# Second attention of a two-layer graph network: one addition moved from VectorE to GpSimd, its two readers one step later

## The reference, cut to what matters

```python
a = ex / denom[tgt]
msg = (v[src] + e) * a[..., None]
out = jax.ops.segment_sum(msg, tgt, num_segments=n).reshape(n, HID)
x_r = h @ Wskip + bskip
beta = jax.nn.sigmoid(jnp.concatenate([out, x_r, out - x_r], axis=-1) @ Wbeta)
return beta * x_r + (1.0 - beta) * out          # h of the next step, then batch norm over all nodes
```

## Time and profile before

| | |
|---|---|
| median of three runs | 2253.55 us |
| profiled execution, its own time | 2257.49 us |
| span of its instructions | 2255.7 us |
| busy: PE, DVE, ACT, POOL | 87%, 73%, 58%, 52% |
| mean granted clock of PE | 0.949 |
| second half of attention 1, first `spread` to last bn_stats | 1277.4 to 1401.7 us of the span |
| POOL instructions in that stretch | none |

### The profile page before, as it was taken

How to read it: one execution, slowest core, us unless ns; L and a number is a source line. 1 busy time by engine, 2 the same in 40 slices (tenths; PEclk the granted TensorE clock), 3 DMA queues, 4 the chain that set the end, 5 groups by cost and what they waited for, 6 DMA issues and landing times. The chain is left out here.

```text
span 2255.7 us, 31284 instructions
## 1 busy us (share of the span) xinstructions
PE 1957.4 (87%) x7584; PEld 1106.5 (49%) x7584; DVE 1641.7 (73%) x3493; ACT 1311.9 (58%) x2509; POOL 1183.5 (52%) x919
## 2 busy tenths in 40 slices
PE   3899999989996889888588697599998999599997
PEld 2444444444332444444233232477776777355554
DVE  6799999967698799999233698577776776355553
ACT  3688888852221677777233211577877776466662
POOL 7566566428840433333688000555555555688885
PEclk9899999999798999999789899699999999799999
DMA  6888888744121999999544132999999997755531
GB/s 174 248 264 258 252 255 258 228 144 95 28 54 32 330 367 363 371 356 337 153 116 122 42 110 87 278 308 319 322 321 305 317 322 221 181 123 127 129 102 26
DMA packets 285896, 476.09 MB, mean 211 GB/s; under 512 B 82181, under 2 KB 158866, under 8 KB 285593
## 3 DMA queue, kind: packets, MB, share of 16 engines
q1 hardware_dynamic: 235494, 440.94, 62.0%
q0 software_dynamic: 46400, 33.03, 7.3%
q10 hardware_dynamic: 3824, 0.13, 0.1%
HBM read 272.01 MB, written 202.55 MB: 210 GB/s over the span
## 5 line engine op out<-in xcount | busy, mean ns | idle before, releaser
L390 POOL DMA_INDIRECT first_x<-in_x,first_index x200 | 262.9, 1315 | 158.5 <-ACT first_xn L584 86.0
L1003 POOL TENSOR_TENSOR last_xh<-last_xin,last_hin 125x512 f32<-125x512 f32 x100 | 127.1, 1272 | 223.7 <-DMA last_xin<-in_x 223.7
L785 POOL DMA_INDIRECT second_entry<-node_map,second_si x100 | 129.9, 1299 | 203.3 <-DVE src_row L800 180.3
L1087 PE MATMUL last_psH<-last_g,W2a 128*128 128x500 f32 x400 | 190.9, 600 | 24.4 <-DVE last_hid L1049 24.3
L1096 PE MATMUL last_psO<-W2b,last_hid 128*125 128x128 f32 x1600 | 190.9, 273 | 0.0
L1096 PEld LDWEIGHTS last_psO<-W2b,last_hid 128*125 128x125 f32 x1600 | 182.5, 188 | 0.9 <-issue 0.9
L203 ACT ACTIVATE last_xn<-last_x,last_nb,last_rstd 125x128 f32<-125x128 f32 x400 | 164.0, 487 | 0.1
L544 PE MATMUL first_psW<-first_h,W_in 128*128 128x500 f32 x300 | 153.5, 594 | 0.0
L1138 POOL DMA_INDIRECT out<-elast_o,elast_ends x100 | 128.5, 1285 | 45.1 <-issue 43.5
L856 PE MATMUL second_psZ<-second_h,gate_h 128*128 128x500 f32 x200 | 105.6, 610 | 51.5 <-DVE second_y L811 28.9
L1382 ACT ACTIVATE att_sig<-att_bank,gate_b 128x500 f32<-128x500 f32 x50 | 33.9, 678 | 196.0 <-PE att_bank L1325 196.0
(11 more groups left out here) (288 smaller groups left out, 5079.1 us busy)
## 6 DMA issues: line engine op xcount, KB each, us to landing
hT<-first_h SPq DMA_DIRECT2D x100, 250.0 KB
yT<-first_y SPq DMA_DIRECT2D x100, 250.0 KB
second_yin<-yT SPq DMA_DIRECT2D x50, 500.0 KB
second_hin<-hT SPq DMA_DIRECT2D x50, 500.0 KB
yT<-second_y SPq DMA_DIRECT2D x50, 500.0 KB
last_yin<-yT SPq DMA_DIRECT2D x50, 500.0 KB
first_x<-in_x SPq DMA_DIRECT2D x100, 224.0 KB
h_rows<-second_rows SPq DMA_DIRECT2D x50, 448.0 KB
```

Source lines behind the costliest of these rows:

```text
L390: pool.indirect_dma_start(x[:, to % X, j], None, a["x"], bass.IndirectOffsetOnAxis(index[:, end, r % 2, j:j + 1], 0), bounds_check=last_no ...
L785: pool.indirect_dma_start(entry[:, q], None, scratch.node_map, bass.IndirectOffsetOnAxis(si[:, q], 0), bounds_check=last_node, oob_is_err= ...
L1003: pool.tensor_tensor(xh[:, q % 4], xin[:, q], hin[:, q], ALU.add).then_inc(m.xh, 1)
L1087: last = pe.matmul(psH[h][:, 0:CH], w.W2a[:, 0, h * 128:(h + 1) * 128], g[:, q % 2], start=True, stop=True)
```

## The change

In attention 1 the addition dx = dx + o is taken from DVE and given to POOL (`add_out`, after all its gathers). The mask of run ends and the bn_stats become a stage of their own, `end_of_run`, which runs with lag 1 in attention 0 (where it stood) and with lag 2 in attention 1. DVE gets two more waits, in both attentions: the scan of chunk k waits for the sum of chunk k - 2 (`y`), and 1532 waits for the masked result of chunk k - 2 (`yn`).

```diff
+                def add_out(k):
+                    pool.wait_ge(m.gx, made(k))
+                    pool.tensor_tensor(dx[:, k % 2], dx[:, k % 2], o[:, k % 2], ALU.add).then_inc(m.y, 1)
+
                 steps(C, [(0, fetch if l else scatter)])
+                if l == 1:
+                    steps(C, [(0, add_out)])
...
                     dve.wait_ge(m.gated, made(k - 2))
                     dve.wait_ge(m.pv, made(k))
                     dve.wait_ge(m.o, made(k - 1))
+                    dve.wait_ge(m.y, made(k - 2))
                     dve.tensor_tensor_scan(o[:, s], run_cont[:, q, 0:CH], pv[:, s], o[:, 1 - s, CH - 1:CH] if k else 0.0,
                                            ALU.mult, ALU.add).then_inc(m.o, 1)
 
                 def combine(k):
 
                     s, q = k % 2, k % U
+                    dve.wait_ge(m.yn, made(k - 2))
...
-                    dve.wait_ge(m.gx, made(k))
-                    dve.tensor_tensor(dx[:, s], dx[:, s], o[:, s], ALU.add).then_inc(m.y, 1)
+                    if l == 0:
+                        dve.wait_ge(m.gx, made(k))
+                        dve.tensor_tensor(dx[:, s], dx[:, s], o[:, s], ALU.add).then_inc(m.y, 1)
+
+                def end_of_run(k):
+                    s, q = k % 2, k % U
                     dve.wait_ge(m.y, made(k))
                     dve.scalar_tensor_tensor(out=yd[:, k], in0=run_cont[:, q, 1:CH + 1], scalar=-1.0, in1=dx[:, s], op0=ALU.add, op1=ALU.mult).then_inc(m.yn, 1)
                     dve.wait_ge(m.yn, made(k))
                     dve.bn_stats(w.ends[:, k * 6:k * 6 + 6], yd[:, k]).then_inc(m.ystats, 1)
 
-                steps(C, [(0, weigh), (0, total), (1, combine)])
+                steps(C, [(0, weigh), (0, total), (1, combine), (1 + l, end_of_run)])
```

## The result

| | before | changed | ratio, 95% interval |
|---|---|---|---|
| median (runs) | 2254.28 us (7) | 2237.27 us (7) | 0.9935 [0.9909, 0.9961] |
| profiled execution, span | 2255.7 us | 2234.0 us | |
| first gate of attention 1 to the next phase's first bn_aggr (line 637) | 122.26 us | 108.56 us | |
| from there to the end | 851.0 us | 843.9 us | |

The ratio is worth 14.7 us of 2254.28, between 8.8 and 20.5 us by its interval. The changed median of 2237.27 us lies in the forecast range of 2236 to 2246. The stretch that the change touches is read more sharply: 13.70 us shorter, against 13.65 predicted. The two spans differ by another 8.0 us. Of these, 7.1 lie behind line 637 and 0.9 ahead of the first gate. The code from line 637 to the end is the same in the thirteen kernels of this study, and in their traces it took 839.0 to 853.7 us, so 7.1 us there cannot be put down to the change.

A forecast was written before the change was run, and what follows sets the result against it. DVE bounds attention 1 before, PE after: -14.75 us of steps and +1.10 of tail give -13.65, with +0.75 in attention 0 -12.9 us. Forecast median 2240.7 us (-0.57%), its own range 2236 to 2246, overall 2235 to 2253.

The forecast's parts named there:

- DVE sets the old step, PE the new one: Attention 1: the bound passes from DVE at 4.84 us a step to PE at 4.19; chance 0.65.
- PE's pace of 4.19 us: Attention 1: five products of 0.84 us a step, read where PE did not wait yet, carry all gates.
- The short idle time before 1540: Sign expected in attention 1's profile after: DVE briefly idle before 1540, ended by PE or ACT.
- DVE's own step: Attention 1 after the change: DVE's instructions take 4.01 us a step, 4.06 with the added waits.
- The size of a wait: Added DVE wait at the scan, already met: 0.03 to 0.05 us each, bounds nothing and 0.2 us.
- Attention 0: DVE stays the bound there; the added scan wait, 25 times 0.03 us, costs 0.75 us, at most 5.
- POOL's addition: Attention 1: held behind 1557, it ends 2.46 us after 1540's start, before the scan at 2.83.
- The cover: Attention 1: POOL's sum reaches the scan with 0.26 us to spare; another 0.13 us hides under PE's step.
- the second rival: Attention 1: POOL gets in first and holds 1557, DVE's step becomes 5.3 us, total 2266 us; chance 0.09.
- C + 0.81: Attention 1: 0.81 us after 1540's start (C), when POOL can start; a mask starting later would be held 1.25 us.
- The tail: End of attention 1: the last mask waits for POOL, 2.57 us after the last 1532 instead of 1.47; +1.10 us.
- The loads: Attention 1: `run_cont` loads, issued a step later, keep 2.0 us to spare and cost nothing.

The follow-up runs named there:

- e3: Kernel before the change with product 1327 and the waits for it left out in attention 1; ratio 0.9997, step 4.81 us.
- e2: Changed kernel with product 1327 and the waits for it left out in attention 1; ratio to the kernel before 0.9909, step 3.96 us.
- e1: Changed kernel with a wait and three one-column memsets on DVE ahead of each mask in attention 1; ratio to the kernel before 0.995, step 4.22 us.
- the runs with 250 and 500 columns: Changed kernel with an extra POOL addition of that many columns ahead of each add_out in attention 1; ratios to the kernel before 0.9931 and 0.9999.
- e6: Changed kernel with a wait and one 161-column memset on DVE ahead of each mask in attention 1; ratio to the kernel before 0.9941, step 4.31 us.
- e9: Changed kernel with two 161-column memsets, each waited for, on DVE ahead of each mask in attention 1; ratio to the kernel before 1.0074.
- e4: Changed kernel with mask and statistics back at lag 1 in attention 1, the addition still on POOL; ratio to the kernel before 1.0099.

## Why the prediction was right

**DVE sets the old step, PE the new one.** Right, and shown by e3 and e2: the same product is worth 1.2 us of phase before, most of it from elsewhere, and 7.4 us after. PE's pace of 4.19 us, read from the few steps before PE began to wait, held over the phase: the gates of chunks 0 and 24 stand at 1281.56 and 1381.32, 99.76 us apart, for 24 x 4.19 - 0.84 = 99.72. The granted clock was 1.00 from 1290 to 1380. The short idle time before 1540, ended by PE, came as predicted.

**DVE's own step.** 4.01 us and the waits, 4.06 predicted. Worked out from what was measured: 1540 to the mask 0.63 us in e2, as predicted, the gap 0.30 with six waits, so 4.01 + 0.07 = 4.08 us, which e1 shows as well; 3.96 us in e2 with five waits. The size of a wait was off: 0.07 us for `y` as the sixth instead of 0.03 to 0.05, and nothing for it as the fifth. In attention 1 this cost nothing, since PE's step covers it.

**Attention 0** got 0.39 us longer from its first scan to its last statistics (133.34 to 133.73 us), against 0.75 predicted. This term was sized at twice what it measured, and it is made up otherwise. The gap was not 0.23 to 0.26 us but 0.30 in chunks 2 to 10 and 0.19 late. Eight steps are 0.07 us longer, one where the gap turns to 0.19 is 0.42 longer (5.26 us, the scan waiting for PE's 1325), the late ones are 0.01 to 0.02 shorter, and a step of 5.94 us that the kernel before has near the end is 5.58.

**POOL's addition.** Hold behind 1557, end at 2.42 (2.46 predicted) and the scan after it: as worked out. The start at exactly 0.81 us after 1540 is in part luck: 1540 takes 0.74 us there instead of 0.71, and the handoff 0.07 instead of 0.10. The handoff back took 0.13 us to the scan in the runs with 250 and 500 columns and 0.03 at the last mask, for 0.11 predicted. The cover was 0.46 us by the run with 250 columns, for 0.26 on VectorE and 0.13 under PE in the prediction.

**The decision point of the second rival** was mis-sized. I put it at the start of POOL's row, C + 0.81. e6 shows POOL still losing with the mask at C + 0.93, e9 shows it winning with the mask at C + 1.34. The rival's mechanism is real, with 0.57 us of hold in e9, but it was farther from the changed kernel than I gave it. An estimate of where it decides: POOL's row takes 1.24 us alone and ends 1.10 us after the mask that holds it, so it is 0.14 us into its row when it needs what the mask holds. That fits e6, where the mask started 0.13 us into the row and was first, and the earlier trace rows, where 0.31 us was too late. It puts the decision at C + 0.95. No run has a mask between C + 0.93 and C + 1.34, so this is not shown more closely.

**The tail** cost 0.97 us for 1.10 predicted: 0.08 from the handoff, the rest from a POOL row that ended 1.09 us after the mask's instead of 1.15.

**The loads** of `run_cont` never show in the waits: right by the rows, though not tried by itself.

**The total.** Forecast -12.9 us, measured -14.7 by the ratio, with an interval of 8.8 to 20.5; the two stretches that the change touches sum to -13.70 + 0.39 = -13.3 us. From 1532 or 1540 of chunk 0 to that of chunk 24 the traces give -14.70 for -14.75. That the phase agrees to 0.05 us is partly luck, since small errors offset each other: this term is 0.05 us too favourable, the tail 0.13 too large, and 0.03 lie in stretches that the forecast takes as unchanged. The 0.36 us of the long step are in the forecast too, since it subtracts from the end that the kernel before reached with it. That it came out clear of 0.5% in the median was the likeliest case, but the interval's upper end, 0.9961, does not exclude 0.4%.

The Trainium skill, "SBUF — State Buffer", section "Who interferes with whom", says that issue order decides who blocks. e9 agrees: 1.24 us of POOL untouched, 1.24 instead of 0.67 for the mask. e6 adds that the start of POOL's row in the profile is not the moment at which that order is settled.

No version here that does the whole work is faster than the changed kernel clear of the noise. The next gain would have to take work off PE in this phase, and would meet DVE's own 4.08 us a step after 0.11 us: 24 x 0.11 = 2.6 us. e2 got more in the steps, 24 x 0.23 = 5.5 us, only because a wait on DVE went with the product.

## What to carry to other kernels

Moving an instruction from the bounding engine to an idle one pays only if the bounding engine's own next reader is put far enough behind: 5.52 us a step with the reader at once, 4.19 with the reader a step later. Before summing the gain, look for a stretch in which the second-busiest engine does not wait yet; its pace there is the floor (0.65 us a step gained here, not the 0.78 that DVE gave up). And list the instructions of VectorE with two inputs in SBUF around a GpSimd operation. The mask and the addition ran one after the other here, whichever came first, so both must fit the step, and the one with slack should come second. For the scan this is not shown: no POOL addition overlapped one.

## What the runs showed of the hardware that was not expected

- Waits that are long met did not cost VectorE the same each. With the waits at the scan: four 0.20 us of gap, five 0.19 (with `y`) or 0.23 (with `xo`), six 0.30 (with both). Whether the number decides or which ones they are is not shown.
- Three one-column memsets in a row took 0.07 us together, and the mask behind them started 0.77 us after 1540, where an instruction that depends on its forerunner starts 0.75 us after it in the earlier trace rows. Such fillers are next to no delay.
- GpSimd's result let VectorE start 0.03 us after the row's end for the mask (in e4 and at the end of the changed kernel), a third of the 0.11 us in the earlier trace rows, and 0.13 us after it for the scan with its six waits (with 250 and 500 columns more).
- GpSimd's addition, 0.13 us into its row, still waited for a VectorE instruction that started after it; 0.55 us into its row it did not. In the earlier trace rows it was 0.31 us into its row when VectorE had to wait.
